# A graph layer's gathers on GpSimd: SyncE fetches one tile of every fifth block row by row

## The chip, the cores and the metric

The kernel runs on one core of a Trainium2 chip. The metric is the device time of one execution in microseconds; lower is better. The core has TensorE (PE), VectorE (DVE), ScalarE (ACT), GpSimd (POOL) and SyncE (SP), each with an instruction stream of its own, and they meet only through semaphores.

## The reference

12,500 nodes with 128 features, 200,000 edges sorted by destination. Cut to what matters:

```
h = relu(layernorm(x))                                  # 12500 x 128
score = (h[dst] W_Q^T . h[src] W_K^T) / sqrt(128) * exp(-edge_weight)
keep the 16 highest scores of each destination node
alpha = softmax of the kept scores, per destination
agg[dst] = sum over kept edges of alpha * (h[src] W_msg^T)
out = x + relu(h W_self^T + agg)
```

Each edge needs the row `h[src]`, and `src` is random.

## The kernel before

It first writes h to `H_table` in device memory, and the edges' source nodes, slots and decays to `META_table`. Then it goes through B = 100 **blocks** of NB = 125 destination nodes. The edges of a block (2000 on average) lie in up to T = 18 **tiles** of 128 edges. Tile t of a block is a 128 x 128 part of one of NE = 7 buffers `Et[b % NE]`, which the profile calls E (b % 7 = 0, 1), Z (2, 3) and X (4 to 6). Tile 0 is copied from the block before by ScalarE (`share`); tiles 1 to 15 are gathered by GpSimd with one indirect DMA each (`gather`), whose 128 row numbers are a column of `idx`; tiles 16 and 17 are gathered at the head of the block only if it has so many edges. Gather (b, t) below is tile t of block b.

GpSimd is in order. Before gather (b, t) it waits by `landed` for the gather eight tiles back, semaphores `s_gp[t % 8]`: before (b, 6) for (b−1, 14). By `in_step` it also waits until the other engines are no more than a lead behind, which is 79 gathers at first and falls by 3.4 a block to zero at block 24. VectorE does in its iteration b the scores of block b (in five groups, the last with tiles 14 to 17), the choice and the weights of block b−1 and the end of block b−2 (`finish`, mark `fin`). TensorE and ScalarE are staged alike.

SyncE loads and stores. Its round j has, in this order: `meta(j+7)` (one register load from `alrow`, three DMAs of 18 rows from `META_table` to MR), `load_h(j+3)` (hb), `spread(j+3)` (a register load, the broadcast of `D16_table` to the buffers rawi and ewt), `load_x(j)` (xb; waits for `fin` of block j−2) and `store(j-2)` (out, the same wait). The register loads read a number from on-chip memory that becomes the address of a DMA.

## Time and profile before

| | us |
|---|---|
| time, median of 3 runs | 2572.68 (2568.25 to 2587.43) |
| span of the profiled execution, first to last instruction | 2021.2 |
| profiled execution's own time | not given apart from its span |
| GpSimd busy | 1492.9 (74%) |
| VectorE busy | 1485.8 (74%) |
| TensorE busy | 1406.6 (70%) |
| ScalarE busy | 1073.1 (53%) |

The span is what the trace covers. The median is of other executions and holds 551.5 us more, which no view shows. Busy time leaves out the time in which an engine's sequencer issues, waits, or handles registers. SyncE has nothing but such instructions, so it has no busy time and is read from its timeline.

### The profile page before, as it was taken

To read this page: it belongs to the slowest core of one execution; us is meant where nothing else is said; L and a number is where in the kernel's file an instruction comes from. 1 tells how busy PE (TensorE), PEld (TensorE's weight loads), DVE (VectorE), ACT (ScalarE), POOL (GpSimd) and SP (SyncE) were. 2 spreads that over 40 slices of the span, in tenths; PEclk is the share of its full clock that TensorE was granted. 3 is DMA by queue.
4 is the path that set the end of the run, shared out by engine and by line. 5 is a ranking of instruction groups with operands and counts; after the bars stand their busy time and mean duration, and the time that the engine had idled before them with its cause. 6 is when DMAs were issued, how large, how long until landed. Compare 5 with 4: busy or idle time off the path is not lost.

```text
span 2021.2 us, 48472 instructions
## 1 busy us (share of the span) xinstructions
PE 1406.6 (70%) x15219; PEld 1293.2 (64%) x15220; DVE 1485.8 (74%) x5024; ACT 1073.1 (53%) x3376; POOL 1492.9 (74%) x1577
## 2 busy tenths in 40 slices
PE   1157888767767677767767766776777677777776
PEld 0147778667666666666666766666766666666765
DVE  6668999676777767676776867777676767777766
ACT  3767666545555455554545545554554545455553
POOL 7776777777777777777777777777777777777773
PEclk9968999888888887888888889888888987887887
DMA  8832334333333333333333233333333333333321
GB/s 231 281 92 84 115 106 115 98 90 101 86 101 90 97 102 87 102 87 99 90 97 101 87 101 86 101 91 97 102 88 100 89 99 88 99 102 87 100 74 33
DMA packets 120627, 206.05 MB, mean 102 GB/s; under 512 B 32268, under 2 KB 75922, under 8 KB 120172
## 3 DMA queue, kind: packets, MB, share of 16 engines
q0 software_dynamic: 50112, 102.80, 19.8%
q1 hardware_dynamic: 69627, 97.27, 14.8%
q8 instruction: 121, 1.98, 0.4%
q10 hardware_dynamic: 626, 2.84, 0.4%
q14 instruction: 141, 1.16, 0.2%
HBM read 186.34 MB, written 16.44 MB: 100 GB/s over the span
## 4 chain that ended last, share of the span: by engine, by line
DVE 36%; issue 20%; DMA 15%; PE 14%; POOL 6%; ACT 4%; POOLq 2%; SPq 1%; ACTq 0%; DVEq 0%
DVE s L896 10%; DMA X<-H_table,idx 6%; DMA E<-H_table,idx 5%; PE pS L1285 5%; DMA Z<-H_table,idx 4%; DVE Dm L920 4%; DVE X L891 4%; DVE D L789 4%; POOL X L610 3%; PE pU L1278 2%; PE pT L1242 2%; POOL Z L610 2%; POOL E L610 2%; PE pS L1242 2%; ACT X L1149 2%
## 5 line engine op out<-in xcount | busy, mean ns | idle before, releaser
L610 POOL DMA_INDIRECT X<-H_table,idx x662 | 627.6, 948 | 205.8 <-issue 157.6
L1149 ACT ACTIVATE X<-OT,w 128x125 f32<-128x125 bf16 x1792 | 530.0, 386 | 30.7 <-DVE w L970 30.7
L610 POOL DMA_INDIRECT E<-H_table,idx x437 | 414.5, 949 | 141.7 <-issue 110.3
L1121 ACT ACTIVATE OT<-pT 128x512 bf16<-128x512 f32 (+1 forms) x500 | 274.6, 549 | 399.5 <-PE pT L1253 388.3
L610 POOL DMA_INDIRECT Z<-H_table,idx x403 | 382.7, 950 | 123.8 <-issue 92.4
L1253 PE MATMUL pT<-identb,O 125*128 125x128 bf16 x1800 | 212.1, 244 | 306.7 <-DVE X L891 255.5
L1253 PEld LDWEIGHTS pT<-identb,O 125*128 125x128 bf16 x1800 | 133.5, 108 | 358.3 <-issue 274.9
L1242 PE MATMUL pG<-G,O 125*128 125x128 bf16 x3600 | 313.8, 250 | 0.0
L1242 PEld LDWEIGHTS pG<-G,O 125*128 125x128 bf16 x3600 | 275.8, 115 | 0.1
L896 DVE TENSOR_REDUCE s<-X 128x8 f32<-128x1024 f32 x200 | 268.3, 1342 | 0.0
L1285 PE MATMUL pS<-Dm,OT 128*128 128x145 bf16 x1800 | 196.2, 287 | 0.4 <-DVE Dm L920 0.4
L1278 PE MATMUL pU<-X 128*128 128x125 f32 x1512 | 190.0, 281 | 1.5 <-ACT X L1149 0.2
L1278 PEld LDWEIGHTS pU<-X 128*128 128x128 f32 x1512 | 179.2, 195 | 10.5 <-ACT X L1149 9.1
L1285 PEld LDWEIGHTS pS<-Dm,OT 128*128 128x128 bf16 x1800 | 178.6, 129 | 0.6 <-DVE Dm L920 0.6
L1242 PE MATMUL pS<-G,O 125*128 125x128 bf16 x600 | 65.7, 263 | 105.9 <-DVE Dm L920 105.9
L1278 PE MATMUL pU<-X,E 128*128 128x125 f32 x1080 | 134.1, 283 | 0.6
L1278 PEld LDWEIGHTS pU<-X,E 128*128 128x128 f32 x1080 | 129.7, 199 | 3.6 <-ACT X L1149 3.4
L1136 ACT ACTIVATE Os<-pU 125x128 f32<-125x128 f32 x100 | 27.7, 277 | 187.3 <-PE pU L1278 187.3
L1278 PE MATMUL pU<-X,Z 128*128 128x125 f32 x1008 | 126.4, 280 | 1.1
L1265 PE MATMUL pAW<-V,O 125*128 125x6 bf16 x1800 | 60.9, 166 | 92.0 <-DVE V L959 91.3
L1278 PEld LDWEIGHTS pU<-X,Z 128*128 128x128 f32 x1008 | 118.2, 193 | 8.0 <-ACT X L1149 7.6
L1242 PEld LDWEIGHTS pS<-G,O 125*128 125x128 bf16 x600 | 44.1, 116 | 123.3 <-DVE Dm L920 123.3
(197 smaller groups left out, 2488.5 us busy)
## 6 DMA issues: line engine op xcount, KB each, us to landing
rawi<-D_table SPq DMA_DIRECT2D x50, 576.0 KB
ewt<-D_table SPq DMA_DIRECT2D x50, 576.0 KB
X<-H_table,idx POOLq DMA_INDIRECT x662
E<-H_table,idx POOLq DMA_INDIRECT x437
Z<-H_table,idx POOLq DMA_INDIRECT x403
hb<-H_table SPq DMA_DIRECT2D x100, 62.5 KB
xb<-in_x SPq DMA_DIRECT2D x100, 62.5 KB
out<-ob SPq DMA_DIRECT2D x100, 62.5 KB
```

Of the source, the lines that this page charges most:

```text
L610: return eng.indirect_dma_start(out=Et[q][:, t * 128:(t + 1) * 128], out_offset=None, in_=x if b < RAW else H, in_offset=bass.IndirectOffs ...
L789: yield VA.mark(eng.tensor_tensor(D01[q][:, :, :], iota[:, 0:SLOT].unsqueeze(1).to_broadcast([128, T, SLOT]), pA[:, 64:64 + TP].unsqueeze( ...
L891: yield VM.mark(eng.tensor_tensor(junk[:, c0:c0 + n], Et[b % NE][:, c0:c0 + n], gx(g)[:, 0:n], ALU.mult), b, f"s{g}")
L896: yield VM.mark(eng.tensor_reduce(s[:, t:t + n], junk[:, t * 128:(t + n) * 128].rearrange("p (t d) -> p t d", d=128), AX.X, ALU.add), b, f ...
L920: yield VM.mark(eng.tensor_tensor(Dm[:, :, 2 * SLOT:3 * SLOT], D01[b % NI][:, :, :], pL.unsqueeze(2).to_broadcast([128, T, SLOT]), ALU.mul ...
L1121: AT.mark(eng.activation(OT[b % 3][:, q0[g]:q0[g] + GQ[g], :].rearrange("p t n -> p (t n)"), pT[:, 0:GQ[g] * 128], ACT.Copy), b, f"T{g}")
L1149: last = eng.activation(weighted(c)[:, t * 128:t * 128 + NB], OT[c % 3][:, t, 0:NB], ACT.Copy, scale=w[:, t:t + 1])
L1242: last = eng.matmul(gx(g)[:, k * 128:(k + 1) * 128], lhsT=O[b % 3][0:NB, t * 128:(t + 1) * 128], rhs=G3[b % 2][0:NB, i, :], start=(i == 0) ...
L1253: last = eng.matmul(pT[:, k * 128:(k + 1) * 128], lhsT=O[b % 3][0:NB, t * 128:(t + 1) * 128], rhs=identb[0:NB, :], start=True, stop=True)
L1265: last = eng.matmul(pW[:, t, :, :].rearrange("p i v -> p (i v)"), lhsT=O[b % 3][0:NB, t * 128:(t + 1) * 128], rhs=V3[0:NB, :, :].rearrange ...
L1278: last = eng.matmul(pU[:, 0:NB], lhsT=Et[d % NE][:, t * 128:(t + 1) * 128], rhs=weighted(d)[:, t * 128:t * 128 + NB], start=(k == 0 and t ...
L1285: last = eng.matmul(pS[:, 0:3 * SLOT + 1], lhsT=OT[b % 3][:, t, :], rhs=Dm[:, t, 0:3 * SLOT + 1], start=(t == 0), stop=(t == T - 1))
```

## The change

In the blocks b = 8, 13, 18, ..., 98 (`owned(b)`, 19 of them) GpSimd leaves out the gather of tile OWN = 14. SyncE fetches that tile's 128 rows of 512 bytes instead, each with a DMA of its own from `H_table` to one partition, in five rounds of PER = 26 rows (the last 24) in its rounds j = b−5 to b−1. Round k stands after `spread` and before `load_x`. The row numbers come from a new table `SRC_table` (the source nodes as integers, three new DMAs of SyncE in the setup): round k = 0 copies the tile's 128 numbers to `own`, and each round then loads its 26 into registers with one instruction. `landed` waits for the rows' semaphore `s_row` in place of the gather's.

```diff
--- before.py
+++ after.py
@@ -64,9 +64,15 @@
     PIECE = 4
     LEAD = 5
     CP = [1, 1, 1, 1, 1, 5]
+    OWN = 14
+    EVERY = 5
+    FROM = 8
+    PER = 26
 
     H = nc.dram_tensor("H_table", [N, D], f32, kind="Internal").ap()
     D16 = nc.dram_tensor("D16_table", [1, MP], i16, kind="Internal").ap()
+    SRC = nc.dram_tensor("SRC_table", [1, MP], i32, kind="Internal").ap()
+    HF = H.rearrange("n d -> (n d)")
     META = nc.dram_tensor("META_table", [4, MP], f32, kind="Internal").ap()
 
     ctx = ExitStack()
@@ -130,6 +136,7 @@
         alrow = sb("alrow", [1, 128], i32)
         alf = sb("alf", [1, 128])
         cprow = sb("cprow", [1, 128], i32)
+        own = sb("own", [1, 128], i32)
 
         MR = [sb(f"MR{q}", [128, 128]) for q in range(NM)]
         dec_ = [sb(f"dec{q}", [128, TP]) for q in range(NI)]
@@ -243,6 +250,9 @@
         s_er = sem("s_er")
         s_gp = [sem(f"s_gp{k}") for k in range(AHEAD)]
         s_relay = sem("s_relay")
+        s_sc = sem("s_sc")
+        s_own = sem("s_own")
+        s_row = [sem(f"s_row{q}") for q in range(2)]
         s_fl = sem("s_fl")
         s_fg = sem("s_fg")
         s_tick = sem("s_tick")
@@ -275,10 +285,21 @@
         q0 = [sum(GQ[:g]) for g in range(5)]
         p0 = [sum(GP[:g]) for g in range(4)]
 
+        def owned(b):
+            return FROM <= b < B and (b - FROM) % EVERY == 0
+
+        def owned_before(b):
+            return len([c for c in range(b) if owned(c)])
+
         def landed(eng, b, t):
             if b >= 0:
                 k = t % AHEAD
-                eng.wait_ge(s_gp[k], 16 * ((1 if k < 2 else 2) * b + t // AHEAD + (0 if k == 1 else 1)))
+                if t == OWN and owned(b):
+                    n = owned_before(b)
+                    eng.wait_ge(s_row[n % 2], 16 * 128 * (n // 2 + 1))
+                else:
+                    less = owned_before(b) if k == OWN % AHEAD else 0
+                    eng.wait_ge(s_gp[k], 16 * ((1 if k < 2 else 2) * b + t // AHEAD + (0 if k == 1 else 1) - less))
 
         class Once:
 
@@ -296,7 +317,7 @@
 
         moments = ["bn", "sum", "dif", "mean", "sq", "m2", "var"]
         shares = ["rstd", "nmr", "n", "h"]
-        vn = ["zero", "ident", "identb", "mr0", "msf", "pad16", "pad", "rawd", "neq", "c1", "winr", "win", "wini", "val", "scan",
+        vn = ["zero", "ident", "identb", "mr0", "msf", "pad16", "pad", "msz", "rawd", "neq", "c1", "winr", "win", "wini", "val", "scan",
               "ctmp", "carry", "slot", "cnt2", "rb", "rbrow", "rbf", "al", "alf", "step", "cp"]
         vn += [f"{k}0" for k in moments + shares]
         vn += [f"{k}1" for k in moments]
@@ -567,9 +588,31 @@
             load_h(1)
             for p, q in RUNS:
                 eng.dma_start(META[1, 0:M].rearrange("(p r) -> p r", r=RUN)[p:q, :], rawd[p:q, 1:]).then_inc(s_late, 16)
+            for p, q in RUNS:
+                eng.dma_start(SRC[0, 0:M].rearrange("(p r) -> p r", r=RUN)[p:q, :], src2[p:q, :]).then_inc(s_sc, 16)
+            VS.wait(eng, "msz")
+            eng.dma_start(SRC[0, M:MP].rearrange("(t e) -> t e", e=128), ms[:, :]).then_inc(s_sc, 16)
             meta(LEAD + 1)
             load_h(2)
             spread(2)
+
+            def own_rows(b, k):
+                n = owned_before(b)
+                if k == 0:
+                    if n == 0:
+                        eng.wait_ge(s_sc, 48)
+                    r = eng.value_load(alrow[0:1, b:b + 1], min_val=0, max_val=M)
+                    eng.dma_start(own[:, :], SRC[0:1, bass.ds(r + OWN * 128, 128)]).then_inc(s_own, 16)
+                    PM.wait(eng, b - NE, "agg3")
+                    AC.wait(eng, b - NE, "cp")
+                    eng.wait_ge(s_own, 16 * (n + 1))
+                lo, hi = PER * k, min(PER * (k + 1), 128)
+                _, rows = nc.values_load_multi_w_load_instructions(own[0:1, lo:hi], engines=[mybir.EngineType.SP], min_val=0, max_val=N - 1,
+                                                                     skip_runtime_bounds_check_because="source nodes of the input")
+                for p in range(lo, hi):
+                    eng.dma_start(Et[b % NE][p:p + 1, OWN * 128:(OWN + 1) * 128],
+                                  H[bass.ds(rows[p - lo], 1), :]).then_inc(s_row[n % 2], 16)
+
             for j in range(B):
                 if j + LEAD + 2 < B:
                     meta(j + LEAD + 2)
@@ -577,6 +620,9 @@
                     load_h(j + 3)
                 if j + 3 < B:
                     spread(j + 3)
+                for k in range(EVERY):
+                    if owned(j + EVERY - k):
+                        own_rows(j + EVERY - k, k)
                 load_x(j)
                 if j >= 2:
                     store(j - 2)
@@ -665,6 +711,8 @@
                             eng.reg_add(total, total, 16)
                 eng.reg_add(total, total, 16)
                 for t in range(1 if b else 0, SURE):
+                    if t == OWN and owned(b):
+                        continue
                     if t in (AHEAD, AHEAD + 1) and b > 0:
                         landed(eng, b - 1, t)
                     elif t >= AHEAD and t != AHEAD + 1:
@@ -716,6 +764,8 @@
             PS.wait(eng, "src0")
             VA.mark(eng.tensor_copy(idx[0][:, :], pA[:, 0:TP]), 0, "idx")
             VS.mark(eng.tensor_scalar(pad[:, :], pidx[0:4, 0:1].to_broadcast([4, CAP]), -1.0, None, ALU.mult), "pad")
+            VS.wait(eng, "msf")
+            VS.mark(eng.memset(ms[:, :], 0), "msz")
             eng.wait_ge(s_dst, 48)
             VS.wait(eng, "zero")
             VS.mark(eng.tensor_copy(rawd[:, :], rawi[:, :]), "rawd")
```

SyncE's instructions at the end of its round j = 2 and in the part of round j = 3 around the new place, before the change (MR, hb, rawi, ewt, xb: buffers that the DMAs fill):

```order
L525 DMA hb0<-H_table 125x128 [waits PB]
L519 TENSOR_LOAD alrow [waits VO]
L519 ISA x2
L520 REGISTER_ALU
L520 DMA rawi<-D16_table 128x2304
L530 DMA xb1<-in_x 125x128 [waits VF]
L534 DMA out_0<-ob1 125x128 [waits VF]
```

and after it, from the same load of hb on, up to the third of 26 rows:

```order
L546 DMA hb0<-H_table 125x128 [waits PB]
L540 TENSOR_LOAD alrow [waits VO]
L540 ISA x2
L541 REGISTER_ALU
L541 DMA rawi<-D16_table 128x2304
L604 TENSOR_LOAD alrow [waits s_sc]
L604 ISA x2
L605 ISA
L605 DMA own<-SRC_table 1x128
L610 TENSOR_LOAD own [waits s_own,AC,PM]
L613 ISA
L613 DMA E1<-H_table 1x128
```

Between the broadcast (L520, now L541) and the load of xb (L530, now L551) there now stand the fetch of `own`, one load of registers, and a register instruction and a DMA for each row.

GpSimd's instructions from tile 12 of block 8 (E1) to tile 8 of block 9 (Z), before the change; the branches around tiles 16 and 17 are left out:

```order
L610 DMA E1<-H_table,idx2 128x128 [waits PG,s_gp4]
L610 DMA E1<-H_table,idx2 128x128 [waits PG,s_gp5]
L610 DMA E1<-H_table,idx2 128x128 [waits PT,s_gp6]
L610 DMA E1<-H_table,idx2 128x128 [waits PG,s_gp7]
...
L610 DMA Z<-H_table,idx3 128x128 [waits s_g,s_gp5,PM]
L610 DMA Z<-H_table,idx3 128x128 [waits PM,s_gp6]
L610 DMA Z<-H_table,idx3 128x128 [waits AU,s_gp7]
```

and after it:

```order
L656 DMA E1<-H_table,idx2 128x128 [waits PG,s_gp4]
L656 DMA E1<-H_table,idx2 128x128 [waits PG,s_gp5]
L656 DMA E1<-H_table,idx2 128x128 [waits PG,s_gp7]
...
L656 DMA Z<-H_table,idx3 128x128 [waits s_g,s_gp5,PM]
L656 DMA Z<-H_table,idx3 128x128 [waits PM,s_row0]
L656 DMA Z<-H_table,idx3 128x128 [waits AU,s_gp7]
```

The gather of tile 14 is gone, and gather (9, 6) waits for `s_row0`, all 128 rows of block 8, where it waited for `s_gp6`.

## Rows read from the trace of the kernel before

**Rows 1.** The page: span, busy time by engine, GpSimd's busy tenths in 40 slices.

```profile
span 2021.2 us, 48472 instructions
...
PE 1406.6 (70%) x15219; PEld 1293.2 (64%) x15220; DVE 1485.8 (74%) x5024; ACT 1073.1 (53%) x3376; POOL 1492.9 (74%) x1577
...
POOL 7776777777777777777777777777777777777773
```

**Rows 2.** Waits of GpSimd from 166 us on: waiter <- releaser: us, times, longest.

```profile
POOL X L610 <- issue: 145.0, 472, 1.2
```

**Rows 3.** GpSimd's timeline: start, us, operation; Z begins block 9, tile 1.

```profile
204.75 0.95 POOL L610 DMA_INDIRECT Z<-H_table,idx  x1 [0.30 <-issue]
...
209.75 0.94 POOL L610 DMA_INDIRECT Z<-H_table,idx  x1 [0.30 <-issue]
210.99 0.94 POOL L610 DMA_INDIRECT Z<-H_table,idx  x1 [0.30 <-issue]
```

**Rows 4.** Window view of the gathers' line: stretch, length, GpSimd's busy time and count.

```profile
166.00:1991.80 1825.80, 1379.41 (x1454) 0.86 0.33 96
```

**Rows 5.** SyncE's timeline: load_x(2), spread(6); load_h(7), spread(7); load_x(6), spread(10), load_x(7).

```profile
169.60 0.30 SPq L530 DMA_DIRECT2D xb<-in_x  x1
...
174.34 0.36 SPq L520 DMA_DIRECT2D rawi<-D_table  x1
...
201.64 0.30 SPq L525 DMA_DIRECT2D hb<-H_table  x1
202.93 0.36 SPq L520 DMA_DIRECT2D rawi<-D_table  x1
...
227.25 0.31 SPq L530 DMA_DIRECT2D xb<-in_x  x1
...
231.50 0.36 SPq L520 DMA_DIRECT2D rawi<-D_table  x1
241.57 0.30 SPq L530 DMA_DIRECT2D xb<-in_x  x1
```

**Rows 6.** SyncE's timeline at mid-span: one round.

```profile
1004.55 0.32 SPq L530 DMA_DIRECT2D xb<-in_x  x1
...
1006.81 1.25 SPq L513 DMA_DIRECT2D MR<-META_table  x3
...
1024.89 0.30 SPq L530 DMA_DIRECT2D xb<-in_x  x1
```

**Rows 7.** Waits of SyncE's queue: us in total, times, longest.

```profile
SPq L530 <- DVE ob L873: 1391.2, 98, 20.6
```

**Rows 8.** Views of single lines: duration ns minimum/median/maximum, first and last start.

```profile
L513 SPq MOVE MR<-META_table x300: 29/29/38, 26.1 to 1852.1; - x150
L513 SPq DMA_DIRECT2D MR<-META_table x300: 277/283/711, 26.1 to 1852.1; - x150
L513 SPq FUSED_REGOPS  x200: 37/42/47, 26.5 to 1852.0; - x100
...
L500 SPq DMA_DIRECT2D X<-in_x x6: 247/252/253, 7.4 to 52.1; - x6
...
L519 SPq TENSOR_LOAD <-alrow x100: 276/517/1466, 78.0 to 1925.2; - x100
...
L1130 ACTq TENSOR_LOAD <-cprow x99: 272/278/473, 110.5 to 1975.1; - x99
```

**Rows 9.** Timelines of SyncE and TensorE near 92 us: a load and its use.

```profile
91.28 0.66 SPq L525 DMA_DIRECT2D hb<-H_table  x2
...
93.83 0.44 PE L1232 MATMUL pBC<-ident,hb 125*128 125x125 f32 x1 [25.05 <-DMA hb<-H_table]
```

**Rows 10.** GpSimd's timeline at its end: tiles 6 and 15 of block 99.

```profile
1979.57 0.94 POOL L610 DMA_INDIRECT E<-H_table,idx  x1 [0.30 <-PE pT L1253]
...
1990.82 0.94 POOL L610 DMA_INDIRECT E<-H_table,idx  x1 [0.30 <-issue]
```

**Rows 11.** The page, SyncE's DMA queue: packets, MB, share of 16 engines' span.

```profile
q1 hardware_dynamic: 69627, 97.27, 14.8%
```

## The prediction

> **What bounds the kernel now.** I read the busy line and the busy digits first, then what GpSimd waits for, then the timelines of GpSimd and SyncE. No engine looks full: GpSimd is busy 74% [rows 1]. But its digit is 7 in nearly every slice, and the page counts only the 0.94 us of a gather. Its timeline shows one gather every 1.25 us, with 0.30 us before each that nobody else ends [rows 2, 3]. From 166.0 to 1991.8 us, 1454 gathers at 1.25 us fill 1817.5 of 1825.8 us [rows 4], and no GpSimd wait for another unit in that stretch stands high in the list: 472 of them end in "issue", longest 1.2 us [rows 2]. So from block 7 on GpSimd's issue rate sets the end. A gather saved is worth 1.25 us there, and a stall of GpSimd costs its full length.
>
> The second thing to see is that GpSimd is **far ahead at first**. Gather (block 9, t=6) starts at 210.99 us [rows 3]; SyncE has by then passed the broadcast of its round j=4 (202.93), and its round j=7 ends its D16 broadcast only at 231.50+0.36=231.86 us [rows 5]. In this stretch the other engines go at 14.3 us a round (241.57−227.25) [rows 5] and catch up with GpSimd; later they go at GpSimd's pace, 1024.89−1004.55=20.3 us there [rows 6].
>
> The third is SyncE's room. It waits 1391.2 us in 98 waits for `fin`, 14.2 us a block [rows 7]. Its own work, from load_x to the end of the broadcast, is 231.86−227.25=4.6 us [rows 5].
>
> **What goes.** 19 blocks (8, 13, ..., 98) lose one gather: 19×1.25=23.7 us, all on the bounding path [rows 3, 4]. One lies ahead of gather (9,6), the other 18 (22.5 us) behind it.
>
> **What SyncE gets.** Each j from 3 to 97 carries one round: four of 26 rows, one of 24, with one load of as many registers. A row is one fused register instruction and one DMA, like the second and third META loads of `meta`: 42 ns, a 29 ns move, and the DMA. Three such DMAs take 1.25 us together, the first of them up to 0.32 us, as xb's does [rows 6], so two more take 0.93 and the pitch is 0.465 us for 18 partitions. A DMA of one partition takes 252 instead of 283 ns [rows 8]. That gives **0.435 us a row**: 26 rows 11.3, 24 rows 10.4, 128 rows 55.7 us. The DMA alone, 0.25 us, is the lower bound; 0.48 the upper.
>
> **The load of 26 registers** has no like in this trace. A load of one register takes 278 ns on ScalarE and 276 ns at best on SyncE, where it follows a DMA and has a median of 517 ns [rows 8]. Its first register costs 0.52+0.05 us. Each further one, m, lies between nothing (all come with the first) and 0.23 us (a whole load less a register instruction, 276−42). I take m=0.14 us, half of a whole load: that a load by itself is seven times a register instruction speaks for a round trip to SBUF in it, and nothing in the trace shows two in flight. 25 more registers are then 3.5 us a round, 123 of them 17.2 us a block owned.
>
> Round k=0 also loads alrow, computes, and fetches `own`: from broadcast to the next DMA, the steps are those between hb's DMA and the broadcast, 202.93−201.94=0.99 us [rows 5]; from its issue to its use is at most 2.5 us (hb issued at 91.28, used at 93.83) [rows 9]; less the 0.24 by which a load after a wait is shorter, 3.3 us. Its waits for `agg3` and `cp` of block b−7 are for the round two back; I count them as covered by the same time.
>
> **The cycle of five rounds on SyncE** is 5×4.65+3.3+5×0.57+55.7+123m = 85.1+123m us (4.65 is the 4.6 of own work and a gap). With m=0.14 it is 102.3 us. GpSimd's five blocks take (1979.57−210.99)/18−1.25=97.0 us after the change [rows 3, 10]. The two are equal at m=0.097. So with my value **SyncE becomes the bound**: 14.2 us of wait a block are filled by 11.3+0.6+3.5+0.7=16.1 us.
>
> **Who waits for it.** By the order of instructions the row semaphore of block 8 stands at GpSimd's gather (9,6), and so at gather 6 of each block after an owned one; ScalarE's `share` and VectorE's last score group wait for it too, later. Round k=4 of block 8 comes after the broadcast of j=7. Time of its landing: round 0 starts at 174.34+0.36=174.70, +0.99+2.5 to the landed `own`, +0.3 for the load, +11.3: 189.8; each of the next three +4.65+0.57+11.3: 239.4; the last +4.65+0.57+10.4, +2.2 after its last issue to land: 257.2 us. To this come the 123 further registers, 17.2 us: 274.4 us. GpSimd, there at 209.75, stands for 65 us. Its lead is gone and is not given back, because behind it there is no idle time to fill.
>
> From there each owned block's rows land 102.3 us after the last: 274.4+18×102.3=2116 us for block 98, where gather (99,6) now starts at 1979.57 [rows 10]. **Sum: +137 us.** What follows (the last nine gathers, 30 us of tail) stays. The fifth-block scheme's setup (three more SyncE DMAs near 92 us, a memset) costs nothing: SyncE's load_x(2) waits for `fin` until 169.60 anyway [rows 5]; uncovered it would be 1.2 us, three issues of 0.4. METAs, hb and broadcasts come later behind the rows, but are issued one and a half rounds before their use. The profiled span is 2021.2 us and the median 2572.68: 551.5 us lie outside the span, in no view; the profiled execution's own time is not given. I leave them as they are: 2572.7+137=**2710 us**.
>
> The Trainium skill ("Runtime: NRT & Kernel Launch", Instruction fetch mechanics) speaks against this change: a register load costs about 200 ns per register, even in bulk. It says so of HBM addresses; no row here has more than one register, and one alone takes 276 ns. By it the sum would be the second rival's.
>
> **Rivals.** (1) **Stall only.** m below 0.097: SyncE fits into GpSimd's time and only the first stall stays. With m=0: resumed at 257.5 instead of 210.99, +46.5−22.5=+24 us, 2597; with m=0.09, +11 more, 2608. For it: one instruction, one address pattern. Against: the whole-load price above.
> (2) **Every register a full round trip**, m=0.2: the cycle is 109.7, block 8 lands at 281.8, block 98 at 2256: +277, 2850 us. At m=0.23, the upper end, +347, 2920 us.
> (3) **Not slower: cheap rows.** If a row costs the DMA's 0.25 us only and m=0, the rounds fit into the 14.3 us pace: round 4 of block 8 starts at 231.86+0.57, +6.0, +2.2 to land: 240.6. The stall is 30 us, less 22.5: +8 us, 2580. It decides from a row price under 0.43 us (with m=0). Faster than before by over 1% is nearly shut out: the last rows can't start before 231.86, already 20.9 us behind 210.99, so a gain needs either no dependence at gather (9,6), which the order shows, or the lost lead to be worthless (2549).
> (4) **The rows drain slower than they are issued**: one semaphore count and one 512-byte packet a row. SyncE's queue now spends 14.8%×16×2021.2/69627=0.07 us a packet [rows 11], so it would have to be six times slower; then above 2920.
>
> **How the numbers follow.** SyncE as the bound 0.57 (m up to 0.2: 0.47; above: 0.10), stall only 0.25, cheap rows 0.11, slow draining 0.04, faster 0.03. Forecast 2710. The range takes in cheap rows, stall only and SyncE-bound up to m=0.2: 2578 to 2852, 0.83. Under 1% is what a measurement can't tell from no change, here ±25.7 us: cheap rows and half of stall only lie in it, since that case starts at +24. Same 0.18, slower 0.79, faster 0.03.
>
> **What the profile after would show.** One TENSOR_LOAD of `own` a round: 4.0 us right, 0.5 to 2 us rival 1. Row pitch 0.435 us. GpSimd idle once some 65 us before gather (9,6) (47 in rival 1), then 5 us (102.3−97.0) at each of the 18 blocks after owned ones; with SyncE's `fin` waits near zero. If the `fin` waits still total hundreds of us, SyncE isn't the bound and I am too high. The prediction is wrong altogether if GpSimd passes gather (9,6) near 210, or finds its waits absorbed later.

## The result

The changed kernel takes **2866.18 us** (median, 2861.95 to 2870.57), the kernel before 2573.95 us beside it (2568.25 to 2587.43): ratio 1.112, 95% interval 1.108 to 1.116. It is slower, as forecast, but by 292 us where 137 were forecast, and 14 us above the upper end of the range.

The page of the changed kernel: its span, busy line, GpSimd's and the clock's digits, SyncE's DMA queue, and the chain that ended last by engine and by line.

```profile
span 2865.3 us, 55962 instructions
...
PE 1547.1 (54%) x15219; PEld 1410.7 (49%) x15220; DVE 1485.7 (52%) x5025; ACT 1054.7 (37%) x3376; POOL 1477.1 (52%) x1558
...
POOL 6552453545454545454545455455545554546452
PEclk9868677777777767777777777777767767767677
...
q1 hardware_dynamic: 74620, 99.34, 10.8%
...
SPq 42%; issue 29%; PE 9%; another core or an unknown queue 8%; ACT 5%; DVE 3%; POOL 1%; DMA 1%; POOLq 1%; ACTq 1%; DVEq 0%
SPq L613 24%; SPq L610 7%; SPq L534 3%; PE pU L1328 3%; SPq L532 2%; PE pT L1303 2%; ACT X L1199 2%; ACT OT L1171 2%; SPq L540 2%; PE pG L1292 1%; SPq L541 1%; PE pS L1335 1%; POOL X L656 1%; SPq L546 1%
```

SyncE's queue now holds 42% of the chain, 24% on the row DMAs (L613) and 7% on the own loads (L610). GpSimd's digits are 4 and 5 instead of 7 [rows 1]: it does 19 gathers less in 844 us more. The other engines' digits fell with it; no engine is full.

GpSimd's waits in the changed kernel (us in total, times, longest). The DMAs without `idx` are SyncE's rows:

```profile
POOL X L656 <- issue: 182.2, 507, 6.3
...
POOL Z L656 <- DMA E<-H_table: 80.7, 3, 58.5
...
POOL X L656 <- DMA X<-H_table: 72.8, 5, 22.2
POOL E L656 <- DMA X<-H_table: 64.1, 3, 37.7
...
POOL Z L656 <- DMA Z<-H_table: 37.3, 3, 13.1
POOL E L656 <- DMA E<-H_table: 30.9, 3, 13.6
POOL X L656 <- DMA Z<-H_table: 28.2, 2, 15.1
```

80.7+72.8+64.1+37.3+30.9+28.2=314.0 us in 19 waits, one before gather 6 behind each owned block. No wait of this kind is there before. The first is the one forecast; GpSimd's timeline shows it at gather (9,6), where [rows 3] has no gap:

```profile
254.83 0.94 POOL L656 DMA_INDIRECT Z<-H_table,idx  x1 [1.39 <-PE pU L1328]
314.27 0.94 POOL L656 DMA_INDIRECT Z<-H_table,idx  x1 [58.50 <-DMA E<-H_table]
315.52 0.94 POOL L656 DMA_INDIRECT Z<-H_table,idx  x1 [0.31 <-issue]
```

But it is followed by 37.7 and 22.2 us, and then by 5 to 15 at each owned block to the end. SyncE's room is gone; its `fin` wait of [rows 7] is now

```profile
SPq L551 <- DVE ob L923: 36.3, 3, 22.5
```

22.5 us before block 8's first rows, 13.5 in the last round, and 0.3 between. So **SyncE is the bound**, as forecast. VectorE's last score group waits for the same rows; the view of L613 says of it:

```profile
  DVE X L941: 355.6, 19
```

Both wait for the same last row, so the two don't add up.

What SyncE does is in its timeline, at block 8's third to fifth round and in mid-span (compare [rows 5, 6]; L541 is the D16 broadcast, L551 the load of x):

```profile
262.37 0.36 SPq L541 DMA_DIRECT2D rawi<-D_table  x1
264.81 10.56 SPq L613 DMA_DIRECT2D E<-H_table  x26
...
280.20 0.36 SPq L541 DMA_DIRECT2D ewt<-D_table  x1
286.06 10.56 SPq L613 DMA_DIRECT2D E<-H_table  x26
...
300.99 0.36 SPq L541 DMA_DIRECT2D rawi<-D_table  x1
303.00 10.05 SPq L613 DMA_DIRECT2D E<-H_table  x24
...
1418.76 14.97 SPq L613 DMA_DIRECT2D X<-H_table  x26
...
1460.68 23.43 SPq L613 DMA_DIRECT2D X<-H_table  x26
...
1498.06 20.90 SPq L613 DMA_DIRECT2D X<-H_table  x26
```

Two things are to be seen. The same 26 rows take 10.56 us here and 15 to 23 us there. And the step from broadcast to first row, in which the own load lies, is 2.08 us in the third round, 5.50 in the fourth and 1.65 in the fifth, for as many registers. The line view of L610 (ns minimum/median/maximum) has the same spread, and that of L613 shows single row DMAs of over 1 us beside the usual 0.23:

```profile
L610 SPq TENSOR_LOAD <-own x95: 457/2011/5299, 211.9 to 2797.3; - x95
```

```profile
L613 SPq MOVE X<-H_table x1024: 1/29/775, 326.4 to 2546.3; - x171
L613 SPq DMA_DIRECT2D X<-H_table x1024: 2/228/1395, 327.1 to 2546.4; - x171
```

### Two paces

The spans of after and of before can't be set against each other as they stand: the trace of before is of an execution of 2021.2 us, the times are of 2573. The first experiment ran the kernel before unchanged with a profile. Its time has two levels: about 2565 us on some chips (all timed runs of the result among them) and 2025 on others, the same in all runs on one chip; the profile of before, by its span, is of the second kind. No chip was used on two occasions, so whether it is the chip or its state at the time isn't told apart. Ratios below are always between runs on one chip.

### The profile page after: what moved, and what is told of

Read it like the earlier page. It is cut to its first block, busy times and chain, and to the rows that moved or that the text cites. A ratio compares the mean times of both kernels' runs of the same rounds, so it can differ in the third digit from the quotient of the medians.

```text
span 2865.3 us, 55962 instructions
## 1 busy us (share of the span) xinstructions
PE 1547.1 (54%) x15219; PEld 1410.7 (49%) x15220; DVE 1485.7 (52%) x5025; ACT 1054.7 (37%) x3376; POOL 1477.1 (52%) x1558
## 3 DMA queue, kind: packets, MB, share of 16 engines
q1 hardware_dynamic: 74620, 99.34, 10.8%
## 4 chain that ended last, share of the span: by engine, by line
SPq 42%; issue 29%; PE 9%; another core or an unknown queue 8%; ACT 5%; DVE 3%; POOL 1%; DMA 1%; POOLq 1%; ACTq 1%; DVEq 0%
SPq L613 24%; SPq L610 7%; SPq L534 3%; PE pU L1328 3%; SPq L532 2%; PE pT L1303 2%; ACT X L1199 2%; ACT OT L1171 2%; SPq L540 2%; PE pG L1292 1%; SPq L541 1%; PE pS L1335 1%; POOL X L656 1%; SPq L546 1%
## 5 line engine op out<-in xcount | busy, mean ns | idle before, releaser
L1303 PE MATMUL pT<-identb,O 125*128 125x128 bf16 x1800 | 243.0, 270 | 882.6 <-ACT OT L1171 453.3
L1303 PEld LDWEIGHTS pT<-identb,O 125*128 125x128 bf16 x1800 | 149.0, 118 | 942.8 <-ACT OT L1171 484.3
L1013 DVE TENSOR_REDUCE we<-pAW 128x36 f32<-128x108 f32 x100 | 27.0, 270 | 608.3 <-remote 431.0
L1292 PE MATMUL pG<-G,O 125*128 125x128 bf16 x3600 | 338.9, 261 | 3.0 <-issue 2.9
L1292 PEld LDWEIGHTS pG<-G,O 125*128 125x128 bf16 x3600 | 298.0, 122 | 3.9 <-issue 3.8
L1328 PE MATMUL pU<-X 128*128 128x125 f32 x1512 | 208.2, 292 | 27.9 <-issue 22.9
L1335 PE MATMUL pS<-Dm,OT 128*128 128x145 bf16 x1800 | 211.4, 300 | 5.8 <-issue 5.8
L1335 PEld LDWEIGHTS pS<-Dm,OT 128*128 128x128 bf16 x1800 | 193.6, 136 | 7.4 <-issue 7.4
L941 DVE TENSOR_TENSOR X<-X,pT 128x512 f32<-128x512 f32 x42 | 28.8, 685 | 205.5 <-DMA X<-H_table 143.4
L1292 PE MATMUL pT<-G,O 125*128 125x128 bf16 x1200 | 112.4, 255 | 25.8 <-issue 23.9
```

The lines of the kernel that those rows point to most:

```text
L1292: last = eng.matmul(gx(g)[:, k * 128:(k + 1) * 128], lhsT=O[b % 3][0:NB, t * 128:(t + 1) * 128], rhs=G3[b % 2][0:NB, i, :], start=(i == 0) ...
L1303: last = eng.matmul(pT[:, k * 128:(k + 1) * 128], lhsT=O[b % 3][0:NB, t * 128:(t + 1) * 128], rhs=identb[0:NB, :], start=True, stop=True)
L1328: last = eng.matmul(pU[:, 0:NB], lhsT=Et[d % NE][:, t * 128:(t + 1) * 128], rhs=weighted(d)[:, t * 128:t * 128 + NB], start=(k == 0 and t ...
L1335: last = eng.matmul(pS[:, 0:3 * SLOT + 1], lhsT=OT[b % 3][:, t, :], rhs=Dm[:, t, 0:3 * SLOT + 1], start=(t == 0), stop=(t == T - 1))
```

## The experiments

Besides time, each run was read by one sum: GpSimd's waits for row DMAs, as above, less the gathers saved at the chip's gather pitch (the time from one gather to the next, 1.60 or 1.26 us, below). "Sum" in the tables is how far these two terms alone would move the time of before, in us; "moved" is how far it moved, against the median of before on that chip.

### The kernel before on a chip of the slower pace (e0_before)

No edit. Expected: 

> The kernel before, unchanged, for its trace: the trace of before has a span of 2021.2 us while its timed runs take 2572.68, and the changed kernel's span (2865.3) is within 2 us of its time. Theory A (the forecast's: 551.5 us lie outside the span): span about 2021 us again, one gather each 1.25 us without a break. Theory B (the timed executions are slower inside than the one traced; the changed kernel's trace has pauses of about 2 us on GpSimd between gathers, some 5 us a block in blocks where GpSimd doesn't wait for rows): span about 2570 us, those pauses in it, some 25 us a block.

Time 2573.52 us, span 2571.8. So there are 1.7 us outside the span, not 551.5. The page:

```profile
span 2571.8 us, 48472 instructions
...
PE 1539.8 (60%) x15219; PEld 1419.8 (55%) x15220; DVE 1489.9 (58%) x5024; ACT 1052.4 (41%) x3376; POOL 1499.5 (58%) x1577
...
PEclk9968777787787777777777787777777777777777
```

GpSimd's gathers take the same 0.95 us and mostly the same 1.25 us pitch as in [rows 3], but every few gathers there is a pause of 2 to 3 us:

```profile
1291.00 0.94 POOL L610 DMA_INDIRECT E<-H_table,idx  x1 [0.30 <-issue]
1292.25 0.95 POOL L610 DMA_INDIRECT E<-H_table,idx  x1 [0.30 <-issue]
1295.62 0.95 POOL L610 DMA_INDIRECT E<-H_table,idx  x1 [2.42 <-remote]
...
1303.21 0.95 POOL L610 DMA_INDIRECT E<-H_table,idx  x1 [0.30 <-issue]
1306.78 0.95 POOL L610 DMA_INDIRECT E<-H_table,idx  x1 [2.62 <-DVE idx L787]
```

SyncE has such stretches too: its three META DMAs, 1.25 us in [rows 6], take

```profile
1279.33 2.90 SPq L513 DMA_DIRECT2D MR<-META_table  x3
...
1302.64 3.16 SPq L513 DMA_DIRECT2D MR<-META_table  x3
```

Inside such a stretch SyncE's instructions, whatever they are, come in steps of about 0.7 us (some of 1.4), one to a few at each step. The window view from gather (9,1) to the last gather (length, GpSimd's busy time and count, granted clock) gives the pitch: 1787.1/1423=1.256 us in the profile of before,

```profile
204.70:1991.80 1787.10, 1350.11 (x1423) 0.86 0.33 96
```

2281.8/1423=1.604 us here,

```profile
257.20:2539.00 2281.80, 1356.23 (x1423) 0.76 0.27 75
```

and in the changed kernel 2579.5/1404=1.837 us:

```profile
248.70:2828.20 2579.50, 1334.10 (x1404) 0.74 0.23 66
```

Less the 314.0 us of waits for rows, that last one is 2265.5/1404=1.614 us: within 1% of the unchanged kernel's on such a chip. **The waits for rows are nearly the whole loss**: +314.0 us, less 19×1.60=30.4, is +283.6; the spans differ by 2865.3−2571.8=293.5. The 10 us left are taken up again at e14. (The tensor clock fell from 0.86 to 0.76 between the paces, where PE is at 55 to 60% and waits; nothing here says that it limits.)

### One part alone, slower pace (e1 to e3; before there 2562.0 us)

Nobody fetches tile 14 of the owned blocks (its old content is used, so the output isn't the reference's):

```diff
                 if t == OWN and owned(b):
-                    n = owned_before(b)
-                    eng.wait_ge(s_row[n % 2], 16 * 128 * (n // 2 + 1))
+                    pass
...
-                for k in range(EVERY):
-                    if owned(j + EVERY - k):
-                        own_rows(j + EVERY - k, k)
...
```

Expected: 

> Leaves out tile 14 of the 19 owned blocks altogether: GpSimd doesn't gather it, SyncE doesn't fetch it, nobody waits for it (its old contents are used). The SRC table is still written. It is the gain side of the change alone. Theory A (GpSimd's issue rate is the bound): 19 gathers of 1.25 us less, 2573 - 24 = 2549 us; by theory B each gather is worth the pace of the timed runs, 25 us for 16, about 1.5 us: 2544 us. Rival C (something else sets the pace): 2573 us, no change.

The own loads with one row a round (so 123 of the 128 rows aren't fetched, and keep old content):

```diff
-                    eng.wait_ge(s_row[n % 2], 16 * 128 * (n // 2 + 1))
+                    eng.wait_ge(s_row[n % 2], 16 * EVERY * (n // 2 + 1))
...
-                for p in range(lo, hi):
+                for p in range(lo, lo + 1):
```

Expected: 

> The change with its loads of 26 registers but only the first row of each round fetched (123 of 128 rows of the tile left out, old contents used). The loads of own take 2.0, 5.3, 1.85, 5.3 and 1.4 us in the five rounds of the changed kernel, 16 us a cycle. Theory A (SyncE is the bound and the rows are its larger part): its cycle is 5 x 4.65 + 3.3 + 16 + 5 x 0.4 = 45 us, far under GpSimd's 97: only the first stall of about 25 us stays, 2575 us. Rival D (the loads alone do it, by stalling something that others share): well above 2650 us.

All rows, but from fixed places of H, so without the 26-register loads (the fetched values aren't the reference's):

```diff
-                _, rows = nc.values_load_multi_w_load_instructions(own[0:1, lo:hi], ...)
...
-                                  H[bass.ds(rows[p - lo], 1), :]).then_inc(s_row[n % 2], 16)
+                                  H[97 * p:97 * p + 1, :]).then_inc(s_row[n % 2], 16)
```

Expected: 

> The change without its loads of 26 registers: the same 2432 row DMAs, from fixed rows of H (97 times the partition) instead of the source nodes' rows. Theory A with rows at 0.41 us, as most stand in the changed kernel's trace: SyncE's cycle is 5 x 4.65 + 3.3 + 128 x 0.41 = 79 us, under GpSimd's 97, only the first stall stays: about 2595 us, and the loads are the larger part of the loss. Rival E (a row's mean price of 0.68 us, as in the changed kernel's trace, comes with the row DMAs themselves): cycle 23 + 3 + 87 = 113 us, 2573 + 45 + 18 x 16 - 24 = about 2800 us or more.

| run | time, us | ratio, interval | waits for rows | sum | moved |
|---|---|---|---|---|---|
| e1_left_out | 2533.85 | 0.990, 0.986 to 0.993 | none | −30 | −28 |
| e2_loads_only | 2571.10 | 1.004, 1.000 to 1.008 | 28.5+15.0 | +13 | +9 |
| e3_rows_only | 2611.89 | 1.019, 1.014 to 1.024 | 33.7+19.7 | +23 | +50 |

Loads alone cost 37 us over e1 and rows alone 78, together 115; both at once cost 288 (2826.2−2538.0, e8 and e11 below, on one chip). They don't add, which is how a queue with room behaves: SyncE still waits 960.5 us for `fin` with the loads alone and 554.9 with the rows alone, and both stall GpSimd only at the first two owned blocks. Only the two together use up the room. A cost of each row or load on the other engines would have added up. The times of e1 and e2 are near what was expected; e3 is 17 us over its 2595, and 27 over its sum. A row from a fixed place has no register: its median pitch is 0.294 us in place of 0.412, so the move and the register instruction are 0.12 of it.

### Variants at the faster pace (e4 to e7; before there 2025.6 us)

28 rows a round, so that own loads start at bytes 0, 112, 224, 336, 448, all multiples of 16:

```diff
-    PER = 26
+    PER = 28
```

Expected: 

> The change with 28 rows a round instead of 26 (28, 28, 28, 28, 16), so that each load of registers begins at a multiple of 16 bytes in own. In the changed kernel the loads of rounds 1 and 3, which begin at bytes 104 and 312, take 5.2 and 5.1 us on average, those of rounds 0, 2 and 4 (bytes 0, 208, 416) 1.9, 1.6 and 1.4 us. Theory H (a load reads four registers at a time where its address allows, else one): all loads near 2 us, 6.5 us less of SyncE's cycle, which is the bound: 2866 - 19 x 6.5 = about 2743 us. Rival (the price goes with something else of the round, or SyncE isn't the bound): 2866 us, no change.

Every second owned block only:

```diff
-            return FROM <= b < B and (b - FROM) % EVERY == 0
+            return FROM <= b < B and (b - FROM) % (2 * EVERY) == 0
```

Expected: 

> The change for every tenth block (8, 18, ..., 98), the five rounds as they are. Theory A (SyncE is the bound only because its five rounds take 138 us where GpSimd's five blocks take some 124 in the timed executions): with ten blocks for a tile SyncE keeps up, and what is left is the first stall of GpSimd, 58.5 us in the changed kernel's trace, less 10 gathers of 1.5 us: 2573 + 58 - 15 = 2616 us. Rival G (the loss goes with the number of SyncE's instructions): about half of it is left, 2573 + 147 = 2720 us.

The first owned block is 48:

```diff
-    FROM = 8
+    FROM = 48
```

Expected: 

> The change from block 48 on only (11 blocks: 48, 53, ..., 98). Theory A: no first stall of a GpSimd that is ahead, and from block 48 on SyncE's cycle of 138 us against 124: 10 x 14 = 140 us, less what slack SyncE has at the start and one gather: 2573 + 110 to 140, about 2690 us. Rival I (the loss is the early stall and what it does to the lead of the first blocks): about 2560 us.

As e1 (nobody fetches tile 14), with 78 register instructions more in each round of SyncE in the place of the row work (the 468 operations of the loop become 78 fused ones), and one small fetch that depends on them:

```diff
...
+                    eng.reg_load(spare, alrow[0:1, j:j + 1])
+                    for _ in range(9 * PER):
+                        eng.reg_mul(spare, spare, 3)
+                        eng.reg_add(spare, spare, 1)
...
```

Expected: 

> As e1_left_out (tile 14 of the owned blocks neither gathered nor fetched), with 78 fused register instructions of six operations in each of SyncE's rounds j = 3 to 97, about the number of instructions that 26 rows have, and one small fetch: no row DMAs. Theory A (only SyncE's own time matters): it has room for them, 2534 us as e1_left_out. Rival G (the executions slow down with the number of SyncE's instructions, whatever they do, since all sequencers share something): up to 2800 us.

| run | time, us | ratio, interval | waits for rows | sum | moved |
|---|---|---|---|---|---|
| e4_aligned | 2062.46 | 1.018, 1.016 to 1.020 | 51.3 | +27 | +37 |
| e5_every_tenth | 2076.69 | 1.025, 1.022 to 1.027 | 59.3 | +47 | +51 |
| e6_from_48 | 2012.49 | 0.993, 0.991 to 0.995 | 2.1 | −12 | −13 |
| e7_registers | 2003.91 | 0.989, 0.987 to 0.991 | none | −24 | −22 |

The expectations of these four were written for the slower pace, so only what they say of the kind of loss can be held against the runs. Here there is **one stall, at the first owned block**, and none behind it; with the first owned block at 48 there is next to none (2.1 us). I read that as GpSimd's lead over the others, which is used up by then; the lead itself wasn't varied alone. There the change pays what its gathers are worth, so at this pace the rows as such do no harm. e7 rules out that more instructions on SyncE slow the others at this pace: it saves as much as leaving the tile out can. The own loads with 28 registers:

```profile
L610 SPq TENSOR_LOAD <-own x95: 981/1658/1822, 178.6 to 1982.9; - x95
```

None is near 5.3 us. 28 registers in 1.66 us, from starts at multiples of 16 bytes; in the changed kernel the rounds' starts are bytes 0, 104, 208, 312, 416, and its loads take 2.0, 5.3, 1.8, 5.3 and 1.4 us (medians by round): dear exactly where the start is no multiple of 16. (Four registers read at a time, as the expectation has it, would be one reason; the runs show the prices alone.) That is 0.20 us a register there (5.28/26) and 0.06 here (1.66/28).

### The changed kernel beside its variants, slower pace (e8 to e11; before there 2570.2 us)

e8 is the changed kernel, e9 has the edit of e4, e11 that of e1. e10 has 28 rows and starts at 18:

```diff
-    FROM = 8
-    PER = 26
+    FROM = 18
+    PER = 28
```

Expected, e8: 

> The changed kernel itself, beside its variants on one chip, since the chips of the first two sets of runs differ in pace (the kernel before took 2562 us on one, 2025.6 us on the other). Theory (SyncE is the bound from block 13 on): where the kernel before takes about 2560 us, 2866 us again, and GpSimd stands before gather 6 of every block after an owned one. Where it takes about 2025 us, SyncE's cycle is 5x4.65 of its own, 52 of rows, 15 of own loads, 3 of the first round = 93.5 us against GpSimd's 97: then one stall of about 60 us only, 2070 to 2090 us. Rival (the rows disturb GpSimd wherever the kernel runs, SyncE isn't the bound): the same ratio 1.11 on both paces, so 2250 us on the faster one.

Expected, e9: 

> 28 rows a round in place of 26, so that every own load starts at a multiple of 16 bytes. Theory: own loads take 1.7 us each in place of 1.4 to 5.3, that is 7 us less in a cycle of five rounds. Where the kernel before takes about 2560 us (SyncE the bound) that is worth 18x7=125 us against the changed kernel; where it takes about 2025 us, SyncE isn't the bound and only what comes before block 8's last row counts, 7 us of the stall: 2062 us as before and 10 to 20 under the changed kernel. Rival (own loads are hidden): no difference from the changed kernel on either pace.

Expected, e10: 

> 28 rows a round, and the first owned block is 18 in place of 8: 17 blocks lose a gather. Theory (the stall comes from GpSimd's lead over the other engines, which is about 28 us at block 9 and used up some five blocks later, each gaining 5.3 us on it): a stall of at most 10 us, and on a chip where the kernel before takes 2025 us, 2025-17x1.25+5=2010 us, faster than before by 0.7 to 1%. Where it takes 2560 us the first stall is gone, but SyncE's cycle of 131 us against 124 is not: 16x7=112 less the gathers' 21 leaves 2620 to 2650. Rival (the stall belongs to the first owned block, whichever it is: SRC or own come late): a stall of 50 us before gather (19,6), 2050 us and more.

Expected, e11: 

> Nobody fetches tile 14 of the owned blocks, so the output isn't the reference's: what the change could save at best, on the same chip as the three above. Both theories: 19 gathers at 1.25 us less, 24 us (0.988) where the kernel before takes 2025 us, 28 us (0.989) where it takes 2562.

| run | time, us | ratio, interval | waits for rows | sum | moved |
|---|---|---|---|---|---|
| e8_after_again | 2826.19 | 1.101, 1.094 to 1.109 | 292.5 | +262 | +256 |
| e9_aligned_again | 2746.14 | 1.069, 1.062 to 1.075 | 195.4 | +165 | +176 |
| e10_aligned_from_18 | 2703.00 | 1.054, 1.048 to 1.061 | 135.4 | +108 | +133 |
| e11_left_out_again | 2537.97 | 0.988, 0.982 to 0.994 | none | −30 | −32 |

The changed kernel takes 40 us less here than in the result, 21 of them in waits for rows. Aligned loads give back 80 us, so the own loads are on the path; 125 were expected. Their sum in a cycle of five rounds fell from 15 to 7 us, the cycle itself (from the starts of x's loads, rounds 19 to 94) only from 134.9 to 130.6; the rows' mean pitch rose from 0.655 to 0.670 us, 1.9 us of the missing 4, and the rest is not explained. The later start takes 43 us, which leaves e10 53 us above the upper end of what was expected: the stall of 46.3 us at gather (9,6) is gone, at (19,6) one of 17.8 us is left. What is left in e10 is SyncE's cycle of 130.5 us against GpSimd's 121.4: seven to nine us behind most owned blocks to the end.

### SyncE given room, slower pace (e12 to e14; before there 2563.2 us)

e12 is the changed kernel, e13 has the edit of e5, e14 that of e5 and of e10 together.

Expected, e12: 

> The changed kernel itself, beside the two that follow. Theory (SyncE's cycle of five rounds is longer than GpSimd's where each instruction of SyncE's queue takes longer): 2826 to 2866 us where the kernel before takes about 2570 us; where it takes about 2025 us the cycle is 52 us of rows, 15 of loads, 3 of the first round and 23 of its own, 93 us against 97, and the time 2070 to 2090 us. Rival (the rows slow the other engines, whatever SyncE's room): ratio 1.10 on both, 2230 us on the faster one.

Expected, e13: 

> Only blocks 8, 18, ..., 98 are owned; rounds are as in the changed kernel (26 rows, own loads at any start). Theory (SyncE is the bound): behind an owned block five rounds without rows let SyncE catch up. Where the kernel before takes 2570 us: 10 gathers less (14 us), the first stall (58 us), and at most 5 us at each of the nine later blocks: 2610 to 2660 us. Rival (rows and loads slow the others in proportion to their number): half of what the changed kernel loses, 2570+0.5x(256 to 290)=2698 to 2715 us.

Expected, e14: 

> Blocks 18, 28, ..., 98 are owned, 28 rows a round (own loads at multiples of 16 bytes). Theory: no first stall and no SyncE-bound cycle; nine gathers less, so 2570-9x1.4=2557 us plus at most 3 us at each owned block, 2557 to 2585; on the faster chip 2025-11=2014 us. If the theory is whole, this is no slower than the kernel before on either. Rival (half the rows, half the loss): 2570+0.5x(2703-2570)=2637 us.

| run | time, us | ratio, interval | waits for rows | sum | moved |
|---|---|---|---|---|---|
| e12_after_third | 2829.44 | 1.104, 1.099 to 1.110 | 292.3 | +262 | +266 |
| e13_every_tenth_again | 2671.58 | 1.043, 1.037 to 1.049 | 134.8 | +119 | +108 |
| e14_tenth_aligned_18 | 2592.09 | 1.012, 1.006 to 1.018 | 16.8 | +2 | +29 |

e13 and e14 came out between theory and rival. e13's stalls are 60, 28, and then 3 to 12 us behind seven of the other eight owned blocks. It isn't that SyncE doesn't catch up: its waits for `fin` are

```profile
SPq L551 <- DVE ob L923: 579.7, 35, 56.4
```

and by its timeline they lie in the rounds without rows only, in rounds 8 to 12, 18 to 21, 28, 29, 31 and so on, from the first such round on. SyncE has caught up each time before rows begin again, and falls behind in the five rounds with rows alone (in the changed kernel such five take 137 us against 121.4), so their last rows still come late. A longer rest between owned blocks doesn't help there. Five shorter rounds do: e14, with its loads 8 us shorter, has 12.0 us of stall at its first owned block and then only 2.6 and 2.2.

In e14 the stalls are as good as gone, and yet it is 29 us slower than before where the sum says 2. e10 and e3 have the same surplus (25 and 27), e13 has −11 and e1 and e11 about none. The traces show where these differences lie, though not why: the sum leaves out two things that work against each other.

1. From the last 1300 gathers of each trace, less the waits for rows, a gather's pitch is 1.591 us in e0, 1.588 in e1, 1.594 in e11 and 1.597 in e2 and e13, but 1.620 in e3, 1.612 in e10, 1.611 in e14, 1.609 in e8 and 1.622 in the changed kernel of the result. 0.02 to 0.03 us over 1300 gathers is 26 to 39 us. So at this pace the kernels with many rows slow GpSimd a little outside its waits too, by 1 to 2%.
2. Waits early in the kernel cost less than they last. The first of these 1300 gathers starts at 502.5 us in the changed kernel, and at 430.1 in e1 and 438.3 in e11: 64 to 72 us later, with 96.2 us of waits for rows before it.

e10 and e14 have no early stall, so they show the first alone; in e8 and e12 the two nearly cancel. At the faster pace the pitch is 1.256 us before and 1.260 in e16. One trace stands for each kernel, and e7, which could tell rows from instructions, wasn't run at the slower pace; the cause of both stays open.

### Rows one round earlier, faster pace (e15, e16; before there 2025.9 us)

Four rounds of 32 rows, the fifth empty, first owned block 18; e15 every tenth block, e16 every fifth:

```diff
-    FROM = 8
-    PER = 26
+    FROM = 18
+    PER = 32
...
                 lo, hi = PER * k, min(PER * (k + 1), 128)
+                if lo >= hi:
+                    return
```

Expected, e15: 

> Blocks 18, 28, ..., 98 are owned; the rows come in four rounds of 32, the fifth round is empty. Theory (only late rows cost): the 17 us of stall that the form with rounds of 28 still had go, and nine gathers are saved: 2565-11=2554 to 2565 us where the kernel before takes about 2565, 2014 where it takes 2025. Rival (what that form lost beyond its stalls, some 20 us, is a cost of the rows themselves wherever they stand): 2575 to 2590 us.

Expected, e16: 

> Blocks 18, 23, ..., 98 are owned, four rounds of 32, the fifth empty. Theory (SyncE's cycle as a whole is too long): the empty round gives the rows a start of one round once, then SyncE falls behind all the same, about 8 us an owned block: stalls begin some two owned blocks later than with rounds of 28, so 2680 to 2700 us where the kernel before takes about 2565, and 2004 to 2012 us where it takes 2025. Rival (the fifth round alone is late, SyncE has room): no stalls, 2565-21=2545 to 2570 us.

e15 2016.10 us (0.995, 0.994 to 0.997), e16 **2002.95 us** (0.988, 0.986 to 0.990); neither has a wait for a row. e16's 17 gathers at 1.256 us are 21.4 us, it gained 23.0. It beats both kernels at this pace (on its own chip the kernel before takes 2025.9 us), and equals e7, in which the tile isn't fetched at all. Its own loads:

```profile
L612 SPq TENSOR_LOAD <-own x68: 1871/1883/2052, 323.3 to 1917.5; - x68
```

The start at 18 and the empty fifth round weren't tried apart at this pace. At the slower pace neither kernel was run. SyncE's cycle could be shorter than e10's there by one load at most, so e16 would be expected to lose (an estimate, near e10's 1.05), and e14's surplus isn't told apart by these two.

### The changed kernel at the pace of the profile (e17; before there 2025.3 us)

No edit. Expected: 

> The changed kernel itself. Where the kernel before takes about 2025 us: theory (SyncE's cycle of five rounds fits under GpSimd's 97 us there, so that only block 8's late rows cost): one stall of 59 us before gather (9,6), 19 gathers at 1.25 us less, and 8 us of further gaps as in the variants, 2025+59-24+8=2068 us, ratio 1.02. Rival (it is SyncE's cycle at any pace, or the rows disturb): 1.10, 2230 us. Where the kernel before takes about 2565 us both say 2826 to 2866 us again.

2079.72 us, ratio 1.027 (1.025 to 1.029). Its waits of GpSimd and of SyncE's queue, and its own loads:

```profile
POOL Z L656 <- DMA E<-H_table: 59.8, 1, 59.8
```

```profile
SPq L551 <- DVE ob L923: 48.1, 4, 20.7
```

```profile
L610 SPq TENSOR_LOAD <-own x95: 1436/2010/5328, 178.4 to 2010.1; - x95
```

The theory holds in the main, but not in that SyncE's cycle would fit under GpSimd's. There is one stall of 59.8 us, behind it 9.6 us in seven short waits. The sum is 69.4−23.9=+46, measured +54. The window from the end of the stall gives 1778.6/1399=1.271 us a gather, 1% over the kernel before:

```profile
271.00:2049.60 1778.60, 1324.56 (x1399) 0.84 0.33 95
```

SyncE's `fin` waits are down to 48.1 us, one of 20.7 before block 8's first round and the rest at the end, and five of its rounds take 97.9 us, as many as in the kernel before at this pace. With a gather less they could take 1.26 us less, 96.6, and in e16, where SyncE has room, they take 96.3. From 300 to 1990 us SyncE waits for nothing but its own fetches of `own`, some 2.4 us in most cycles, beside 1.9 us in all. VectorE waits for rows at 18 owned blocks:

```profile
  DVE X L941: 118.2, 18
```

So SyncE is the bound at this pace as well, but only by some 1.3 us a cycle: over 18 cycles that takes back about what the saved gathers gave. The slower gathers behind the stall are the same loss seen from GpSimd, 1399×(1.271−1.256)=21 us, 9.6 of them in waits for rows. The 118.2 us of VectorE's waits cost no more than that.

## Why the prediction was wrong

**Right: the mechanism.** SyncE fills its room and becomes the bound; GpSimd stands before gather 6 behind owned blocks; the first stall is the long one. At the profile's pace the stall was forecast at 65 us with the gathers resuming at 274.4; e17 has 59.8 and 269.81. A gather saved is worth its pitch (e1, e7, e11). Nothing of the change's setup shows. (The forecast's own numbers, 2116 less 1979.57, give 136 us and not 137.)

**The step that failed** is the one on the time outside the span: "551.5 us lie outside the span, in no view; [...] I leave them as they are". They lie inside. At the pace of the timed runs the span is 2571.8 us, and the queues have stretches in steps of 0.7 us. That does less to a gather (1.256 to 1.604 us, ×1.28) than to a queue that issues many short instructions: a row's mean pitch goes from 0.421 us (e17, 56 of 2337 steps over 0.5 us) to 0.657 (the changed kernel, 856 of 2292; both from the starts of all rows, steps over 2.6 us left out), ×1.56. So SyncE's cycle of five rounds, forecast at 102.3 us against 97.0, is 136.9 against GpSimd's 5×24.6−1.6=121.4 (123.0 us for five rounds in e0). Its parts, by the trace: rows 128×0.657=84, own work 5×5.8=29, own loads 15, and 9 us for the first round's fetch, waits and gaps. 15.5 us behind at each of 18 owned blocks is 279 us, beside 314−58.5=255.5 measured: GpSimd and the others were not quite at its heels all the time.

**The terms of the sum.** At the profile's pace every one was near: a row 0.435 us forecast, 0.411 median and 0.421 mean; the own loads 5×0.57+17.2=20 us a cycle forecast, 15.9 measured. With these the cycle is 5×4.65+3.3+128×0.421+15.9=96.4 us, not 102.3; e17 has 97.9, against 96.6 for GpSimd. Rival 1, the stall alone, comes nearer there than the main case: it forecast 2597 to 2608 over 2572.7, that is +24 to +35 us, measured +54, the main case +137. The rest is the stall of 59.8 us in place of 46.5 to 58, and the 21 us of slower gathers behind it. So SyncE is the bound at both paces, but the 5.3 us a cycle of the forecast were 1.3 at the profile's pace and 15.5 at the slower one. That the loss on the timed chips was of the forecast's kind, a stall and then some us at each owned block, was luck: two errors stood against each other, the cycle too long and the pace left out, and the second was larger.

**m**, 0.14 us as half of a whole load, came near the mean of two prices (0.13) by luck: 0.06 us a register at starts of 16-byte multiples and 0.20 elsewhere. The Trainium skill's figure ("Runtime: NRT & Kernel Launch", Instruction fetch mechanics: about 200 ns per register, also in bulk) agrees with the loads of 5.28 us and not with those of 1.4 to 2.0. By it all loads would have cost 26 us a cycle (an estimate, 128 registers at the page's figure); 15 were measured.

**The range** was made of prices of rows and registers alone. No part of it stood for the pace, although the time of before, 27% over the span, said that the profile wasn't of such a run. Rival 4 (rows drain slowly) is out: the first stall ends 1.2 us (the changed kernel) and 1.4 us (e17) behind the end of block 8's last row issue; 2.2 were forecast. Each row went as one packet of 512 bytes and one of 4: SyncE's queue has 74620 packets with the rows and 69718 in e1, 2×2451 more for 2432 rows and 19 fetches of `own`.

## What to carry to other kernels

Set the profile's span beside the timed median first. Where they differ by much, the profile is of a run at another pace, and a queue that issues many short instructions may lose more by it than the engine that it must keep up with (here ×1.56 against ×1.28): ask for the room of each queue at the slower pace, too. A helper queue that has just enough room is a cliff: here the same program costs 3% on one chip and 10 to 11% on another. Give it the work late, where nobody has a lead to lose, in pieces that leave the last round free (e16 does both and is 1.2% faster at the faster pace; at the slower it wasn't run); and start register loads at multiples of 16 bytes.

## What the runs showed of the hardware

- **A load of several registers has two prices**: 26 registers from byte 104 or 312 of a partition 5.28 us, from byte 0 or 208 some 2.0 and 1.8, 24 from byte 416 1.4; 28 from multiples of 16 1.66; 32 from multiples of 128 1.88.
- **This kernel has two paces**, and no run tells whether the chip makes them or its state at the time: about 2025 us on three of the chips and in the profile of before, about 2565 on three others and in the timed runs of the result, each the same in all its runs. At the slower one SyncE's queue has stretches, 2.4 to 2.9 us on average, in steps of 0.7 us: 88 of them in the kernel before (e0), 8% of the span, and 240 in the changed one (e8), where it is seldom idle, a quarter of the span (at least two steps of 0.6 to 0.8 us, with at most 0.1 us between); at the faster pace it has 3 (before) and 4 (e17). GpSimd pauses for 2 to 3 us, as shown above for e0. More instructions don't make such stretches at the faster pace: 78 more a round (e7) left 5. What does at the slower one is not settled.
- **A DMA of one row of 512 bytes** issued from SyncE with its row in a register takes 0.41 us of the queue, 0.29 with a fixed row; the last of 24 is there 1.2 to 1.4 us behind its issue.
